# Attention on one Trainium2 core: the score and maximum products cut into halves of 64 weight columns, issued maximum first, with one signal for both readers

## The reference

```python
q, k, v = (to_heads(q), to_heads(k), to_heads(v))
dots = jnp.einsum('bhid,bhjd->bhij', q, k) * scale
attn = jax.nn.softmax(dots, axis=-1)
out = jnp.einsum('bhij,bhjd->bhid', attn, v)
```

## Time and profile before

| | us |
|---|---|
| median of 3 runs | 2634.01 (2625.93 to 2658.01) |
| the profiled execution | 2648.98 |
| its span, first to last instruction | 2647.2 |
| TensorE busy in the span | 2134.6 (81%) |
| VectorE busy | 1323.2 (50%) |
| ScalarE busy | 1139.9 (43%) |
| mean granted TensorE clock | 0.86 |

### The profile page before, as it was taken

How to read it: one execution, slowest core, us unless ns; L and a number is a source line. 1 busy time by engine, 2 the same in 40 slices (tenths; PEclk the granted TensorE clock), 3 DMA queues, 4 the chain that set the end, 5 groups by cost and what they waited for, 6 DMA issues and landing times. The chain is left out here.

```text
span 2647.2 us, 40358 instructions
## 1 busy us (share of the span) xinstructions
PE 2134.6 (81%) x14306; PEld 962.7 (36%) x14306; DVE 1323.2 (50%) x3515; ACT 1139.9 (43%) x2082; POOL 210.5 (8%) x238
## 2 busy tenths in 40 slices
PE   8975788888888888886758999970755998599999
PEld 4134122222222222211544544430324996345454
DVE  0036867777677777740124443437876443333331
ACT  0012066666666666664114454430521331254544
POOL 0021000000000000000000000003310133100000
PEclk9976589999899989987558999995876997699999
DMA  6825402121221212001110000000000000000000
GB/s 108 149 80 180 86 21 42 22 44 23 45 39 36 40 27 41 14 10 42 66 57 1 1 1 1 1 2 2 0 0 3 1 2 1 22 5 9 5 9 9
DMA packets 60311, 82.61 MB, mean 31 GB/s; under 512 B 26555, under 2 KB 45396, under 8 KB 57068
## 3 DMA queue, kind: packets, MB, share of 16 engines
q1 hardware_dynamic: 57036, 71.60, 12.6%
q0 software_dynamic: 3104, 8.72, 0.9%
HBM read 53.16 MB, written 27.14 MB: 30 GB/s over the span
## 5 line engine op out<-in xcount | busy, mean ns | idle before, releaser
L532 ACT ACTIVATE b_prob<-b_p_s 128x512 f32<-128x512 f32 x1104 | 590.2, 594 | 361.1 <-PE b_p_s L661 316.8
L546 DVE TENSOR_REDUCE b_m<-b_p_m 128x1 f32<-128x1024 f32 x512 | 602.4, 1219 | 215.7 <-PE b_p_m L608 214.7
L661 PE MATMUL b_p_s<-b_q,b_k 51*128 51x512 bf16 x1024 | 365.5, 420 | 120.1 <-DVE b_m L546 97.3
L608 PE MATMUL b_p_m<-b_k,b_q 48*128 48x512 bf16 x1024 | 374.7, 430 | 46.6 <-DMA b_k<-qk_scr 25.5
L688 PE MATMUL b_p_o<-b_prob,b_v 128*32 128x512 f32 x2304 | 340.9, 667 | 0.0
L661 PEld LDWEIGHTS b_p_s<-b_q,b_k 51*128 51x128 bf16 x1024 | 82.9, 96 | 509.1 <-DVE b_m L546 256.9
L1124 ACT ACTIVATE d_hidden<-d_p_z 128x704 f32<-128x704 f32 x192 | 135.5, 755 | 145.1 <-PE d_p_z L1028 144.8
L1124 ACT ACTIVATE n_hidden<-n_p_z 128x704 f32<-128x704 f32 x192 | 135.2, 755 | 127.8 <-PE n_p_z L1028 127.8
L1242 DVE TENSOR_TENSOR d_xg<-d_xd,d_p_c 128x352 f32<-128x352 f32 x192 | 91.3, 517 | 181.2 <-PE d_p_c L1017 181.2
L1242 DVE TENSOR_TENSOR n_xg<-n_xd,n_p_c 128x352 f32<-128x352 f32 x96 | 49.9, 520 | 203.4 <-PE n_p_c L1017 203.4
L1028 PE MATMUL d_p_z<-d_xg,d_w 64*128 64x352 f32 x768 | 144.0, 494 | 0.0
(11 more groups left out here) (317 smaller groups left out, 2584.2 us busy)
## 6 DMA issues: line engine op xcount, KB each, us to landing
xt<-in_x SPq DMA_DIRECT2D x16, 1024.0 KB, 11.7
v_scr<-a_vw SPq DMA_DIRECT2D x8, 1152.0 KB, 4.8
b_v<-v_scr SPq DMA_DIRECT2D x8, 1152.0 KB, 12.2
c_sums<-sum_scr SPq DMA_DIRECT2D x8, 1056.0 KB, 5.8
sum_scr<-b_sums POOLq DMA_DIRECT2D x32, 256.0 KB, 2.3
qk_scr<-a_qk_part SPq DMA_DIRECT2D x24, 264.0 KB, 2.9
b_q<-qk_scr SPq DMA_DIRECT2D x96, 66.0 KB
b_k<-qk_scr SPq DMA_DIRECT2D x16, 198.0 KB
```

The source lines that it names most:

```text
L532: nc.scalar.activation(prob[:, U % PR_RING, 0:w], p_s[:, U % S_RING, 0:w], ACT.Exp, scale=float(D) ** -0.5).then_inc(exp_done, 1)
L546: nc.vector.tensor_reduce(m3[:, x, 0:1], p_m[:, s, :, :].rearrange("p k n -> p (k n)"), axis=AX.X, op=ALU.max).then_inc(rows_free, 1)
L608: last = nc.tensor.matmul(out[:, k, :], q_st[s][r, i, t * P:t * P + P], k_st[s][r, i, k * WIDE:k * WIDE + WIDE], start=True, stop=True)
L661: last = nc.tensor.matmul(out, k_st[s][r, q, jt * P:jt * P + P], q_st[s][r, q, a * WIDE:a * WIDE + WIDE], start=True, stop=True)
```

## The change

1. A score product and a full maximum product, of 128 weight columns each, become two products of 64 weight columns, into output partitions 0 to 63 and 64 to 127. The pieces of the text keys (L619), the text-query scores (L669) and the transposes stay at 128 (or 33) weight columns, the L633 and L664 products at 32.
2. In a unit, the pieces' products come before the score's. From the first unit on (`ALONE`) a maximum product signals nothing; the score's last product signals `scored`, and VectorE waits for the unit's value of `scored` instead of `rows_full`.
3. The waits of all pieces of a unit come first, then the score's wait, then the products. In units with two pieces the second piece's wait thus comes before the score and the first piece.
4. The generator that yields pieces becomes a list, `STEPS`, with `share(U)` naming those of unit U; which piece falls to which unit stays as it was.

```diff
+        def share(U):
+            upto = [ALONE + (PIECES + 1) * j + (PIECES + 1) * u // US for j, u in (divmod(U, US), divmod(U + 1, US))]
+            return range(min(upto[0], len(STEPS)), min(upto[1], len(STEPS)))
...
+            def rows_there(X):
+                if X < ALONE_X:
+                    dve.wait_ge(rows_full, X + 1)
+                else:
+                    dve.wait_ge(scored, pair_of[X] + 1)
...
+                if x < FULL_ROWS:
+                    i, t = divmod(x, FULL)
+                    for e in range(0, P, 64):
+                        last = nc.tensor.matmul(out[e:e + 64, k, :], q_st[s][r, i, t * P + e:t * P + e + 64], k_st[s][r, i, k * WIDE:k * WIDE + WIDE],
+                                                start=True, stop=True)
...
+                if n < ALONE and k + 1 == parts:
+                    last.then_inc(rows_full, 1)
...
-                    last = nc.tensor.matmul(out, k_st[s][r, q, jt * P:jt * P + P], q_st[s][r, q, a * WIDE:a * WIDE + WIDE], start=True, stop=True)
+                    for e in range(0, P, 64):
+                        last = nc.tensor.matmul(out[e:e + 64, :], k_st[s][r, q, jt * P + e:jt * P + e + 64], q_st[s][r, q, a * WIDE:a * WIDE + WIDE],
+                                                start=True, stop=True)
...
-                    upto = AHEAD + (PIECES + 1) * j + PIECES + ((PIECES + 1) * (u + 1)) // US
-                    if done < upto:
-                        next(rows, None)
-                    score_ready(US * j + u)
-                    score(j, u)
-                    if done < upto:
-                        next(rows, None)
-                        done += 1
-                    while done < upto:
-                        next(rows, None)
-                        next(rows, None)
-                        done += 1
+                    U = US * j + u
+                    for n in share(U):
+                        rows_ready(n)
+                    score_ready(U)
+                    for n in share(U):
+                        rows(n)
+                    score(j, u)
```

More of the change, by code:

```diff
@@ L443, in attend_stage @@
         block = c.enter_context(nc.Block())
[L445 to L451, removed]
+        TURN = MS
+        STEPS = []
+        for j in range(NQ):
+            for x in range(MS):
+                if x == TURN_AFTER and j >= 1:
+                    STEPS.append((j - 1, TURN, 0, 1))
+                parts = 2 if x < FULL_ROWS or x == FULL_ROWS + 1 else 4 if x == FULL_ROWS else 1
+                STEPS += [(j, x, k, parts) for k in range(parts)]
+        STEPS.append((NQ - 1, TURN, 0, 1))
+        PIECES = 2 * FULL_ROWS + 4 + 2 + 1
+        ALONE = PIECES + 2 * LEAD
+        def share(U):
+            upto = [ALONE + (PIECES + 1) * j + (PIECES + 1) * u // US for j, u in (divmod(U, US), divmod(U + 1, US))]
+            return range(min(upto[0], len(STEPS)), min(upto[1], len(STEPS)))
+        slot_of = {(j, x): X for X, (j, x, k, parts) in enumerate(step for step in STEPS if step[2] == 0)}
+        pair_of = {slot_of[STEPS[n][:2]]: U for U in range(NQ * US) for n in share(U) if STEPS[n][2] + 1 == STEPS[n][3]}
+        ALONE_X = min(pair_of)
         def load_quad(sp, b, p):
@@ L567, in turned @@
             def turned(j):
-                X = turn_index(j)
-                dve.wait_ge(rows_full, X + 1)
+                X = slot_of[j, TURN]
+                rows_there(X)
                 if j >= 1:
@@ L587, in _, with rows_ready, rows @@
         def _(pe):
-            def rows_of_quad(j):
+            def rows_ready(n):
+                j, x, k, parts = STEPS[n]
+                X = slot_of[j, x]
+                if x == 0 and k == 0:
+                    pe.wait_ge(half_in[j // HG % 2][j % HG], HALF_IN * (j // HG // 2 + 1))
+                if x == TURN:
+                    pe.wait_ge(max_step, 6 * j + 6)
+                if k == 0 and X >= 2:
+                    pe.wait_ge(rows_free, X - 1)
+            def rows(n):
+                j, x, k, parts = STEPS[n]
                 b, p = divmod(j, HG)
@@ L592, in rows_of_quad @@
                 r = slice(64 * p, 64 * p + KS)
[L593 to L647, removed]
+                out = p_m[:, slot_of[j, x] % 2, :, :]
+                if x < FULL_ROWS:
[3 more added lines that the diff above has]
+                                                start=True, stop=True)
+                elif x == FULL_ROWS:
+                    for y in range(8 * k, 8 * k + 8):
+                        i, t = divmod(y, FULL)
+                        bank, at = divmod(y * QN, 512)
+                        last = nc.tensor.matmul(out[:, bank, at:at + QN], q_st[s][r, i, t * P:t * P + P], k_st[s][r, i, TOK:SEQ],
+                                                start=True, stop=True)
+                elif x < TURN:
+                    lo, w = (k * WIDE, WIDE) if x == FULL_ROWS + 1 else (TOK, QN)
+                    for i in range(QUAD):
+                        last = nc.tensor.matmul(out[32 * i:32 * i + 32, k, 0:w], q_st[s][r, i, TOK:SEQ], k_st[s][r, i, lo:lo + w],
+                                                start=True, stop=True)
+                else:
+                    for a in range(PARTS):
+                        last = nc.tensor.transpose(out[0:ROWS, 0, :].bitcast(BF16)[:, a * P:a * P + P], max_part[:, a, :], g.eye_bf[:])
@@ L697, in weigh @@
                 last.then_inc(pv_done, hi - lo)
[L699 to L710, removed]
-                next(rows, None)
-            done = PIECES + AHEAD
+            for n in range(ALONE):
+                rows_ready(n)
+                rows(n)
             pending = None
```

10 lines of the change are left out of this document (6 added, 4 removed).

## The result

The changed kernel takes 2753.35 us (median of 4 runs, 2736.28 to 2764.64) against 2630.58 us before (4 runs, 2625.93 to 2658.01). The ratio on record is 1.0433, 95% interval 1.0353 to 1.0513: the change makes the kernel 4.3% slower.

The account below looks back on a forecast made before the run. Bound: a ring of latencies between TensorE and VectorE, no engine full. Terms 0.3 + 1.8 + 0.7 + 0.7 = 3.5 us a quad, 56 us, plus 8 for the clock: profiled 2713, median 2700 us (+2.5%), range 2630 to 2835.

Parts of the forecast that it names:

- the turnover beside the text-key pieces: Four units a quad at L619: 64- and 128-column products no longer overlap, 0.63 us a unit instead of 0.22, 1.6 us.
- the trap: Rival: clock falls in units 47 to 68, 12 us a quad in eight or all 16 quads; 2796 to 2892 us; chance 0.25.
- the sum: Likeliest case: 3.5 us a quad plus 0.5 for the clock; 2700 us, own range 2670 to 2730, chance 0.35.
- sign of being wrong: Forecast fails if L619 pieces start together with the scores, or the stage's clock moves over 0.05 either way.
- The ring of latencies: Attend stage: TensorE and VectorE wait for each other, no engine full; four units and one weighing repeat every 3.06 us.
- Halves in pairs: Full products: four quarters run together in 0.22 us; extra loads cost 0.01 us each, 0.3 us a quad (0 to 1.4).
- Order and signal: Piece first, score last: 0.7 us a quad (0 to 1.3); one signal less: counted as nothing.
- ScalarE's later start: In a quad's last 15 units and those of 32-column shapes, the exponential comes later: 0.7 us a quad (0 to 1.3).
- Waits of two-piece units: Units 22, 45, 68: VectorE's wait stands before all products; 0.5 us idle at unit 22, 0.7 us a quad (0.4 to 1.5).
- the low clock at a quad's end: After each quad's end, where the clock falls to 1.2 GHz: somewhat longer low stretches, 0.5 us a quad, 8 us.

Follow-up runs that it names:

- another place of the weighing: Kernel before with maximum products 15 instead of 16 pieces ahead and two-piece units 29, 49, 51 instead of 22, 45, 68: 0.9708.
- halves everywhere: Kernel before, its order, signals and waits kept, with every product of 128 weight columns cut into halves of 64: 1.0148.
- order and waits together: Kernel before with whole products, pieces before the score and changed waits; each tile's last piece still signals VectorE itself: 0.9977.
- the halves alone: Kernel before with only scores and full maximum products cut into halves of 64 columns; order, signals and waits as before: 1.0639.
- only the text-key pieces in halves: Kernel before with only the L619 products cut into halves of 64 columns, all full products whole: 1.0787.

## Why the prediction was right, and where it was off

The direction was right, and so were the turnover beside the text-key pieces and the trap as a mechanism; 2753 us lies in the range. It is neither of the two forecasts, though: the sum had 2670 to 2730 for its own, the clock trap 2796 to 2892. By its own sign of being wrong, a clock of the stage that moves by more than 0.05, the sum had failed (0.93 to 0.86), and that the range held is in part luck.

- *The bound.* The ring of latencies stands: another place of the weighing, with the higher clock that came with it, gives 2.9%. Its number was read wrongly. The prediction took all 17 groups of a quad for rings of 3.06 us; in the quad from 602 us the weighings stand 3.06 us apart four times, 3.27 twice, 4.36 once at low clock and 2.39 twice, where they stand between tiles.
- *Halves in pairs.* Right that four quarters run together. The halves take 0.04 to 0.05 us more a ring, with either order (3.06 to 3.10, 3.03 to 3.08, 3.02 to 3.06), about half of the 0.08 that was the upper end for both places. The term as a whole was too small: halves everywhere cost 1.48%, where I had 0.3 us a quad, 5 us (0 to 22). In the profiles the quads carry 1.1 us each of it, 18 us; the span grows by another 9 us after the last copy. The load that I had called no longer than its neighbours is the longer one: 115 ns in the change (groups by line and shape, 420 to 1240 us) and 109 to 110 in halves everywhere, where the clock is as before, against 96:

```profile
L659 PEld LDWEIGHTS b_p_s<-b_q,b_k 51*64 51x64 bf16 x1620 | 82.2, 115 | 21.4 <-issue 13.8
```

- *Halves beside pieces of 128.* Right in place and size: 0.62 us a unit against 0.63 forecast, and VectorE's wait grew by 1.35 us. The Trainium skill's TensorEngine Tiling (Array Packing), Key Properties, says that changing the tiling mode drains TensorE; the trace agrees for 64 against 128 columns, by these 0.62 us.
- *Order and signal.* Wrong in the step. I put 0.7 us a quad on ScalarE's later start and nothing on the signal. The runs show no such cost (0.9977 for order and waits together), even a ring 0.03 us shorter, and 1.7% for the shared signal with whole products. What I missed is that a signal behind the score makes VectorE wait for the unit's longest member, the 16 text-query products: 0.36 us a quad directly, the rest with the clock. The Trainium skill's TensorE: Matmul & The Clock Gate, The cost: per-tile semaphore tail, prices an increment at 26 ns; no run here shows such a gain, with whole products own signals were faster.
- *Waits of two-piece units.* Right in place and kind: 0.51 us of idle time for VectorE at unit 22, 0.5 us forecast. The term of 0.7 us a quad was a little too large, 0.48 measured.
- *The clock.* I held two cases apart, the plain sum and the trap. Both happened. The steps without a long stretch of low clock are 61.5 us, 4.7 more than 56.8, against 4.0 forecast. That agreement hides misses that cancel: the later exponential at 0.7 us and not seen, the signal at nothing and 0.4, and the low clock at a quad's end at 0.5 and, by an estimate, 1.3 (from 573 to 820 us the clock is 0.89, in the quads of the earlier trace rows 0.92; that is 4 us more at 1.2 GHz a quad, at 4.36 us for 3.06). The trap was priced at 12 us a quad, and in the change a long stretch of low clock costs 13, 13 and 10 us: the two steps that share it, less 2 x 61.5. The size was right; the number of such quads was not, three where I had eight or sixteen. Together the long stretches cost 36 us, 1.4%. In the halves alone one costs 21 us over steps of 57.7.

What stays open: why, in the kernel with turnovers, the shared signal keeps the clock up (0.86 against 0.74), while without turnovers it costs 1.7% (whole products), or 1.6% together with the order (halves everywhere). Three of fifteen passages of text-key pieces set off a long stretch of low clock in the change, twelve of thirteen with only the text-key pieces in halves. Whether it falls may hang on small shifts in time; no run here tells that apart.

## What to carry to other kernels

Products on different rows of the array overlapped in these traces only when they had the same number of weight columns. Whoever changes the shape of one partner must change all the partners (that cost 1.5% here), or pay a turnover of 0.1 us twice and the lost overlap, 0.40 us a unit; and a short stretch thinned out like this can bring the clock down for a long one, at several times the price of the stretch itself (1.6 us for the four units, 10 to 21 us for a long stretch of low clock). Before work is cut finer, look at what the accumulating product stands between: moving it from inside a tile to between tiles, and the higher clock that came with it, were worth 2.9% with no new instruction. And a sum that comes out near the measured time proves none of its terms: here several of them missed, and the misses made up for each other.

## What the hardware showed that I hadn't expected

- The clock doesn't follow TensorE's busy time, and a busy TensorE is no sign of a fast one: at the lower clock each product takes longer and fills the time. At the end of the changed stage TensorE is busy 20.00 of 20 us at a clock of 0.51, while with own signals and whole products 6.96 of 10 us busy stood at 1.00 (above, 668 to 678 us):

```profile
1300.00:1320.00 20.00, 20.00 (x90) 3.51 (x90) 0.00 (x0) 9.79 (x20) 0.00 (x0) 0.51 0.00 1
```

- Four changed units of 69 in a quad cost 7.9% of the whole kernel, most of it through the clock: four turnovers at 0.40 us each would be 26 us in 16 quads, 1%.
